# Both normalisations of the first part on ScalarE (scale and bias per row) in place of VectorE

## The chip, the core and the metric

The kernel runs on one core of a Trainium2 chip. Time is the device time of one launch in microseconds (us); lower is better. The core's engines are TensorE (PE; its weight loads are listed as PEld), VectorE (DVE), ScalarE (ACT), GpSimd (POOL) and SyncE (SP), which here only issues DMAs. Each engine runs its own instruction stream in order; the streams meet at semaphores that the program sets by hand.

## The reference

Two transformer layers on 4 x 512 rows of 256 channels, in float32:

```python
x = x + tanh(g_xattn[0]) * L0_xattn(layernorm(x), ctx)     # softmax over 16x16 per row
x = x + tanh(g_ffn[0])   * L0_ffn(layernorm(x))            # shared expert + one of 8 experts
x = x + tanh(g_xattn[1]) * L1_xattn(ctx, ctx, layernorm(x))
x = x + tanh(g_ffn[1])   * L1_ffn(layernorm(x))            # butterfly feed-forward

def layernorm(x, eps=1e-5):
    return (x - mean(x)) / sqrt(var(x) + eps)
```

The first attention is odd: for each row, queries, keys and values are split into 16 heads of 16, and the 16 x 16 scores are formed between the channels of a head, within that one row, so they are no TensorE work: they are element products of 128 x 4096 and sums of these. The change touches the first two layernorms only.

## The kernel before, in words

**Parts.** The first part (first attention, second normalisation, shared expert, router logits) runs over 16 tiles of 128 rows. Then come the routing tables, the expert part (23 tiles of rows gathered by expert), the folding of the butterfly weights, and the last part (second attention and feed-forward). The first part and the routing fill about 335 us of the trace.

**Software pipeline of the first part.** Every engine walks through steps (`sweep_a`). In step k it works on tile k (`t0`: load, first normalisation, keys, values, queries), tile k-1 (`t1`: scores, exp, attention products), k-2 (`t2`: attention sums), k-3 (`t3`: output product, second normalisation, logits) and k-4 (`t4`: shared expert). Steps 0 to 5 are written out, steps 6 to 15 are a hardware loop of two steps per pass, whose waits compare with registers, step 16 is written out, and `drain` holds the rest by hand.

**Order on each engine in a full step.**

- VectorE (`step`, L1445): product for scores L1348, gate product `mult` L1548, score sums L1357, `mult` L1548, residual add L1367, `bn_stats` L1372 for the first normalisation of t0 and the second of t3, row maximum L1387, moments `bn_aggr` L1377 (twice), shift L1396, variance + eps L1382 (twice), sums of exp L1404, XH = normalised rows of t3 (L1414), XN = normalised rows of t0 (L1484), reciprocal L1421, attention sums L1426 (two halves), scaling L1434, residual add L1442.
- GpSimd: the power -1/2 for t3 (L507) and t0 (L514), which makes 1/sqrt(var + eps), and then for t1 the attention products in two halves, each a product L529 and a halving add L531. A half waits until VectorE has read the same half of the tile before (`av_read`).
- ScalarE (`step`, L1151): gelu half (L1135), copy of the transposed attention (L1139), gelu half, copy of keys and values KV (L1165), exp (L1172), copy of transposed XH (L1144), copy of transposed XN (L1178), logits copy (L1149). Gelu and exp need different tables: there is one ACT_TABLE_LOAD ahead of each in a step.
- TensorE: transposes of the attention rows (into bank 3), output product, up product half, keys and values, down product, transposes of XH, transposes of XN, gate product (L766), query product with WQ, up product half of t3.
- SyncE: for tile t, first the store of the XH rows of tile t-5 (`keep_rows`, waits for `xn2_ready`), then the loads of tile t.

A small tensor MV holds for each of the two normalisations (index r = 0, 1) mean, variance, variance + eps and the reciprocal root, one value per row (partition). XN has one buffer, XH two.

**Drain.** After step 16, tiles 14 and 15 still have their second normalisation ahead of them, and tiles 13 to 15 the shared expert; VectorE, TensorE and ScalarE each have a written order. GpSimd computes the root of tile 14 between the two halves of its last attention products, the root of tile 15 at the end, and then issues the loads of butterfly coefficients.

Of the kernel before, what the change touches and what calls it, by code (L numbers as in the profile page):

```python
# [27 lines left out]
P = 128  # L28
# [25 lines left out]
def build(nc, x, ctxT, gates, wq0, wkv0, wo0, wg, wexp, wk1, wv1, wq1, wo1, bv1, bq1, bo1,  # L54
          weT, be, uplow, uphigh, upb, dnlow, dnhigh, wc, bc, db, out):
    with ExitStack() as ctx:
        start, twins = {}, {}

        def sb(name, shape, dt=F32):
            start[name] = (nc.sbuf_base + 31) // 32 * 32  # L60
            return ctx.enter_context(nc.sbuf_tensor(name, shape, dt))
# [13 lines left out]
        def sem(name):  # L75
            return ctx.enter_context(nc.semaphore(name))
# [51 lines left out]
        ST = sb("ST", [P, 2, 6])  # L128
        MV = sb("MV", [P, 2, 4])
        SM = sb("SM", [P, 2, DK])  # L130
        RI = sb("RI", [P, DK])
        LG = sb("LG", [P, T, NE])
        G = sb("G", [P, F])
# [117 lines left out]
        oh_ok h1_done h2_done gelu_done mult_done y_done y_added av_prod av_half recip""".split()  # L251
        s = {n: sem(n) for n in names}
        picked = sem("picked")
        route = sem("route")
        held = sem("held")
        rank_ps = sem("rank_ps")
# [869 lines left out]
        def _(act):  # L1126
            act.wait_ge(wg_in, 48)
            act.activation(TG[:, :], GATE[:, :], ACT.Tanh).then_inc(tanh_s, 1)

            def gelu(t4, hf):  # L1130
                n = 2 * num(t4) + hf
                act.wait_ge(s["h1_done"], n + 1)
                if not first(t4, 1):
                    act.wait_ge(s["mult_done"], n - 1)
                act.activation(G[:, hf * 512:(hf + 1) * 512], PB[6][:, :], ACT.Gelu).then_inc(s["gelu_done"], 1)  # L1135
# [15 lines left out]
            def step(of):  # L1151
                t0, t1, t3, t4 = of(0), of(1), of(3), of(4)
                if t4 is not None:
                    gelu(t4, 0)
                if t3 is not None:
                    attended(t3)
                if t4 is not None:
                    gelu(t4, 1)
                if t0 is not None:
                    n = num(t0)  # L1160
                    act.wait_ge(s["kv_done"], n + 1)
                    if not first(t0, 2):
                        act.wait_ge(s["qk_prod"], n - 1)
                        act.wait_ge(s["av_prod"], 2 * n - 2)
                    act.activation(KV[:, t0[1], :], PB[4][:, :], ACT.Copy).then_inc(s["kv_sb"], 1)  # L1165
                if t1 is not None:
                    n1 = num(t1)
                    act.wait_ge(s["shifted"], n1 + 1)
                    if not first(t1, 2):
                        act.wait_ge(s["av_prod"], 2 * n1 - 2)  # L1170
                        act.wait_ge(s["sums"], n1 - 1)
                    act.activation(PR[:, t1[1], :], SC[:, :], ACT.Exp, scale=float(DK) ** -0.5)\  # L1172
                        .then_inc(s["exp_done"], 1)
                if t3 is not None:
                    normal_rows(t3)
                if t0 is not None:
                    act.wait_ge(s["xT_done"], num(t0) + 1)
                    act.activation(XT[:, :, :].rearrange("p k t -> p (k t)"), PB[1][:, 0:D], ACT.Copy)\  # L1178
                        .then_inc(s["xT_sb"], 1)
                if t3 is not None:  # L1180
                    logits(t3)

            def drain():

                a, b, c = tile(T - 3), tile(T - 2), tile(T - 1)
                gelu(a, 0)
                attended(b)
                gelu(a, 1)
                normal_rows(b)
                logits(b)  # L1190
                gelu(b, 0)
                attended(c)
                gelu(b, 1)
                normal_rows(c)
                logits(c)
                gelu(c, 0)
                gelu(c, 1)
# [137 lines left out]
        def _(dve):  # L1335
# [37 lines left out]

            def moments(t, r, nm):

                hold(s[nm + "_stats"], num(t) + 1)
                dve.bn_aggr(MV[:, r, 0:2], ST[:, r, :]).then_inc(s[nm + "_agg"], 1)  # L1377

# [22 lines left out]
            def exp_sums(t2):  # L1401
# [1 line left out]
                dve.wait_ge(s["exp_done"], num(t2) + 1)  # L1403
                dve.tensor_reduce(SM[:, 1, :], PR[:, t2[1], :].rearrange("p (i j) -> p i j", i=DK),  # L1404
                                  AX.X, ALU.add).then_inc(s["sums"], 1)

            def normal_rows(t3):

                n3 = num(t3)
                dve.wait_ge(s["ln2_rstd"], n3 + 1)  # L1410
                if not first(t3, 2):
                    dve.wait_ge(s["x2T_done"], n3 - 1)
                    dve.wait_ge(xh_out[t3[1]], 16 * t3[0])
                dve.tensor_scalar(XH[:, t3[1], :], X[:, n3, :], MV[:, 1, 0:1], MV[:, 1, 3:4],  # L1414
                                  ALU.subtract, ALU.mult).then_inc(s["xn2_ready"], 1)

            def attended(t2):

# [26 lines left out]
            def step(of):  # L1445
                t0, t1, t2, t3, t4 = of(0), of(1), of(2), of(3), of(4)
                if t1 is not None:
                    scores(t1)
                if t4 is not None:
                    mult(t4, 0)  # L1450
                if t1 is not None:
                    score_sums(t1)
                if t4 is not None:
                    mult(t4, 1)
                if t3 is not None:
                    add_attended(t3)
                if t0 is not None:
                    hold(tile_in[t0[1]], 32 * t0[0] + 32)
                    stats(t0, 0, "ln1")
                if t3 is not None:  # L1460
                    hold(s["x1_ready"], num(t3) + 1)
                    stats(t3, 1, "ln2")
                if t1 is not None:
                    row_max(t1)
                if t0 is not None:
                    moments(t0, 0, "ln1")
                if t3 is not None:
                    moments(t3, 1, "ln2")
                if t1 is not None:
                    shift(t1)  # L1470
                if t3 is not None:
                    guarded(t3, 1, "ln2")
                if t0 is not None:
                    guarded(t0, 0, "ln1")
                if t2 is not None:
                    exp_sums(t2)
                if t3 is not None:
                    normal_rows(t3)
                if t0 is not None:
                    n0 = num(t0)  # L1480
                    dve.wait_ge(s["ln1_rstd"], n0 + 1)
                    if not first(t0, 1):
                        dve.wait_ge(s["xT_done"], n0)
                    dve.tensor_scalar(XN[:, :], X[:, n0, :], MV[:, 0, 0:1], MV[:, 0, 3:4],  # L1484
                                      ALU.subtract, ALU.mult).then_inc(s["xn_ready"], 1)
                if t2 is not None:
                    attended(t2)
                if t4 is not None:
                    add_shared(t4)
# [9 lines left out]
            def drain():  # L1499
# [2 lines left out]
                mult(a, 0)  # L1502
                second_norm(b)
                exp_sums(c)
                normal_rows(b)
                mult(a, 1)
                attended(c)
                add_shared(a)
                mult(b, 0)
                second_norm(c)  # L1510
                normal_rows(c)
                mult(b, 1)
                choices()
                add_shared(b)
# [419 lines left out]
```

## Time and profile before

| | us |
|---|---|
| median of 3 runs (lowest to highest) | 845.53 (844.35 to 851.41) |
| profiled execution | 846.31 |
| its span in the trace | 844.5 |
| busy: TensorE | 748.2 (89%) |
| busy: VectorE | 493.5 (58%) |
| busy: GpSimd | 390.1 (46%) |
| busy: ScalarE | 262.0 (31%) |

Busy shares are means over the whole span; a TensorE that is busy is not TensorE at its peak, since the ends of pipelined matmuls are modelled. "Idle before" in a row is the time its engine stood still ahead of the instruction, with what ended that time. The granted clock (PEclk) is the share of TensorE's full clock of 2.4 GHz; its two levels are 1.2 and 2.4 GHz. Two neighbouring instructions of one engine may overlap by about 0.1 us in the trace.

### The profile page before, as it was taken

To read this page: it belongs to the slowest core of one execution; us is meant where nothing else is said; L and a number is where in the kernel's file an instruction comes from. 1 tells how busy PE (TensorE), PEld (TensorE's weight loads), DVE (VectorE), ACT (ScalarE), POOL (GpSimd) and SP (SyncE) were. 2 spreads that over 40 slices of the span, in tenths; PEclk is the share of its full clock that TensorE was granted. 3 is DMA by queue.
4 is the path that set the end of the run, shared out by engine and by line. 5 is a ranking of instruction groups with operands and counts; after the bars stand their busy time and mean duration, and the time that the engine had idled before them with its cause. 6 is when DMAs were issued, how large, how long until landed. Compare 5 with 4: busy or idle time off the path is not lost.

```text
span 844.5 us, 11772 instructions
## 1 busy us (share of the span) xinstructions
PE 748.2 (89%) x4083; PEld 583.8 (69%) x4083; DVE 493.5 (58%) x821; ACT 262.0 (31%) x498; POOL 390.1 (46%) x326
## 2 busy tenths in 40 slices
PE   4259999999999797999999999999966889899996
PEld 1138877887888686566666666666656789799996
DVE  4889999999999737321211111111165677977652
ACT  1023333333433210122221222222132545456543
POOL 1688998898899844343333333332024141410000
PEclk9569999999999998899999999999998899999999
DMA  7000001000192017104044405000010101000000
GB/s 249 12 19 20 19 20 35 22 19 19 39 308 122 13 47 218 71 19 175 19 169 169 173 26 224 26 21 16 9 38 13 38 26 51 19 18 16 14 14 26
DMA packets 30637, 54.29 MB, mean 64 GB/s; under 512 B 9972, under 2 KB 26148, under 8 KB 29440
## 3 DMA queue, kind: packets, MB, share of 16 engines
q1 hardware_dynamic: 23168, 42.41, 14.2%
q0 software_dynamic: 4112, 8.26, 3.9%
q10 hardware_dynamic: 3312, 3.02, 1.0%
q8 instruction: 29, 0.48, 0.2%
q14 instruction: 16, 0.13, 0.1%
HBM read 46.45 MB, written 7.21 MB: 64 GB/s over the span
## 4 chain that ended last, share of the span: by engine, by line
PE 43%; DVE 11%; issue 6%; ACT 5%; DMA 2%; POOL 1%; ACTq 0%; DVEq 0%; POOLq 0%
PE bank L702 31%; PE bank L961 8%; PE bank L709 3%; DVE SLOT_r L1686 1%; DMA expert_rows<-YS 1%; DVE SLOT L1762 1%; DVE PRODV_r L1686 1%; ACT L1271 1%; POOL PRODQ L552 1%; DVE STC L1747 1%; DVE NM L1797 1%; ACT XS L1271 1%; DMA XS<-normal_rows,INV 1%; ACT SLOT_r L1275 1%; ACT SLOT L1284 1%
## 5 line engine op out<-in xcount | busy, mean ns | idle before, releaser
L702 PE MATMUL bank<-SLOT,XST 128*128 x368 | 164.6, 601 | 0.0
L529 POOL TENSOR_TENSOR PRODV<-SHARED 128x2048 f32<-128x2048 f32 x32 | 144.4, 4513 | 27.9 <-DVE bank L1426 27.9
L702 PE MATMUL bank<-SLOT,HA 128*128 (+1 forms) x624 | 146.2, 388 | 3.3 <-DVE HA L1548 2.0
L702 PEld LDWEIGHTS bank<-SLOT,HA 128*128 128x128 f32 x624 | 120.1, 194 | 38.3 <-issue 12.4
L702 PEld LDWEIGHTS bank<-SLOT,XST 128*128 128x128 f32 x368 | 69.2, 193 | 78.9 <-issue 78.8
L702 PEld LDWEIGHTS bank<-X2T,SLOT 128*128 128x128 f32 x1024 | 121.1, 195 | 1.6
L702 PE MATMUL bank<-X2T,SLOT 128*128 128x128 f32 x1024 | 121.4, 278 | 0.0
L1655 DVE TENSOR_TENSOR SHARED<-bank,G 128x512 f32<-128x512 f32 x46 | 31.8, 692 | 135.0 <-PE bank L702 135.0
L564 POOL DMA_INDIRECT XS<-normal_rows,INV x23 | 23.6, 1025 | 138.6 <-PE bank L709 121.8
L679 POOL TENSOR_TENSOR RS<-VE,MHALF 128x2 f32<-128x2 f32 x16 | 13.2, 823 | 148.3 <-DVE VE L1754 148.3
L1348 DVE TENSOR_TENSOR PRODQ<-bank,SHARED 128x4096 f32<-128x4096 f32 x16 | 70.7, 4418 | 12.6 <-PE bank L702 12.6
L531 POOL TENSOR_TENSOR PRODV<-PRODV 128x1024 f32<-128x1024 f32 x32 | 74.7, 2334 | 2.5
L1357 DVE TENSOR_REDUCE bank<-PRODQ 128x256 f32<-128x4096 f32 x16 | 70.7, 4420 | 0.1
L1646 DVE COPY HA<-bank 128x512 f32<-128x512 f32 x23 | 15.9, 692 | 72.8 <-PE bank L709 72.8
L1220 ACT ACTIVATE G<-bank 128x512 f32<-128x512 f32 x46 | 27.5, 597 | 94.0 <-PE bank L702 94.0
L961 PE MATMUL bank<-SLOT_r,PRODQ_r 128*128 128x256 f32 x256 | 47.8, 286 | 1.4 <-DVE SLOT_r L1686 1.4
L961 PEld LDWEIGHTS bank<-SLOT_r,PRODQ_r 128*128 128x128 f32 x256 | 40.7, 193 | 2.4 <-DVE SLOT_r L1686 1.6
L1226 ACT ACTIVATE YS<-bank 128x256 f32<-128x256 f32 x23 | 8.8, 384 | 106.2 <-PE bank L702 91.0
L1135 ACT ACTIVATE G<-bank 128x512 f32<-128x512 f32 x32 | 19.1, 597 | 69.1 <-PE bank L702 69.0
L702 PE MATMUL bank<-WKV,SHARED 128*128 128x512 f32 x64 | 34.5, 667 | 6.7 <-DMA WKV<-wkv 6.7
L672 POOL DMA_INDIRECT SLOT<-expert_rows,POS x16 | 16.0, 1000 | 50.1 <-DMA expert_rows<-YS 46.4
L1426 DVE TENSOR_REDUCE bank<-PRODV 128x128 f32<-128x1024 f32 x32 | 36.7, 1191 | 0.5 <-POOL PRODV L531 0.5
(243 smaller groups left out, 1368.9 us busy)
## 6 DMA issues: line engine op xcount, KB each, us to landing
SLOT<-wexp SPq DMA_DIRECT2D x9, 3072.0 KB, 11.6
expert_rows<-YS ACTq DMA_DIRECT2D x23, 128.0 KB
X<-x SPq DMA_DIRECT2D x16, 128.0 KB, 2.2
SHARED<-ctxT SPq DMA_DIRECT2D x16, 128.0 KB, 2.3
normal_rows<-XH SPq DMA_DIRECT2D x16, 128.0 KB, 1.7
WET<-ctxT SPq DMA_DIRECT2D x4, 512.0 KB, 8.2
out<-X SPq DMA_DIRECT2D x16, 128.0 KB, 1.7
WET<-weT SPq DMA_DIRECT2D x1, 1024.0 KB, 6.4
```

The lines of the kernel that those rows point to most:

```text
L529: gp.tensor_tensor(o, pr, v, ALU.mult).then_inc(s["av_prod"], 1)
L531: gp.tensor_tensor(o[:, :, :, 0:DK // 2], o[:, :, :, 0:DK // 2], o[:, :, :, DK // 2:DK], ALU.add).then_inc(s["av_half"], 1)
L564: gp.indirect_dma_start(out=XS[:, n % 2, :], out_offset=None, in_=xs, in_offset=bass.IndirectOffsetOnAxis(ap=INV[:, n:n + 1], axis=0))\
L702: last = pe.matmul(dst, lhs(k), rhs(k), start=(k == 0), stop=(k == chunks - 1))
L709: last = pe.transpose(bank[:, k * P:(k + 1) * P], src[:, k * P:(k + 1) * P], IDENT[:, :])
L961: last = pe.matmul(dst, f32r(a), f32r(b), start=(k == 0 and n == 0), stop=(k == chunks - 1 and n == 2))
L1135: act.activation(G[:, hf * 512:(hf + 1) * 512], PB[6][:, :], ACT.Gelu).then_inc(s["gelu_done"], 1)
L1220: act.activation(G[:, hf * 512:(hf + 1) * 512], PB[1 + hf][:, :], ACT.Gelu)\
L1348: dve.tensor_tensor(PRODQ[:, :].rearrange("p (i j h) -> p i j h", i=DK, j=DK), spread(PB[1][:, 0:D].rearrange("p (i o h) -> p i o h", i=DK ...
L1357: dve.tensor_reduce(SCP.rearrange("p (i j) -> p i j", i=DK), PRODQ[:, :].rearrange("p (i j h) -> p i j h", i=DK, j=DK), AX.X, ALU.add)\
L1426: dve.tensor_reduce(aov[:, :, hf * H2:(hf + 1) * H2], PRODV[:, :].rearrange("p (f i h j) -> p f i h j", f=2, i=DK, h=H2) [:, hf, :, :, 0:D ...
L1655: dve.tensor_tensor(HB[:, t1[1], hf * 512:(hf + 1) * 512], PB[3 + hf][:, :], G[:, hf * 512:(hf + 1) * 512], ALU.mult).then_inc(e["b_mult"], 1)
```

## The change

XN and XH are no longer computed by VectorE as (x - mean) * rstd. ScalarE computes them as Identity(rstd * x + bias) with bias = -mean * rstd, both per row. The bias takes two small ScalarE instructions: SHIFT[0] = -mean, and SHIFT[1] = SHIFT[0] * rstd. Semaphores order the three (`mean_neg`, `mean_rstd`), since an instruction may not read what its predecessor has not finished. In a step ScalarE does them behind the exp: the second normalisation (t3), then the first (t0), ahead of its two copies of transposed rows; in the drain behind the second gelu half. VectorE's `moments` now waits until the rows of the tile before have been normalised, since MV is overwritten.

```diff
+        SHIFT = sb("SHIFT", [P, 2, 2])
...
+            def normalise(t, r, nm, dst, signal):
+                n = num(t)
+                act.wait_ge(s[nm + "_agg"], n + 1)
+                act.activation(SHIFT[:, r, 0:1], MV[:, r, 0:1], ACT.Copy, scale=-1.0).then_inc(mean_neg[r], 1)
+                act.wait_ge(mean_neg[r], n + 1)
+                act.wait_ge(s[nm + "_rstd"], n + 1)
+                act.activation(SHIFT[:, r, 1:2], SHIFT[:, r, 0:1], ACT.Copy, scale=MV[:, r, 3:4])\
+                    .then_inc(mean_rstd[r], 1)
+                act.wait_ge(mean_rstd[r], n + 1)
+                act.activation(dst, X[:, n, :], ACT.Identity, bias=SHIFT[:, r, 1:2], scale=MV[:, r, 3:4])\
+                    .then_inc(s[signal], 1)
+            def second_rows(t3):
+                if not first(t3, 2):
+                    act.wait_ge(s["x2T_done"], num(t3) - 1)
+                    act.wait_ge(xh_out[t3[1]], 16 * t3[0])
+                normalise(t3, 1, "ln2", XH[:, t3[1], :], "xn2_ready")
+            def first_rows(t0):
+                if not first(t0, 1):
+                    act.wait_ge(s["xT_done"], num(t0))
+                normalise(t0, 0, "ln1", XN[:, :], "xn_ready")
...
             # ScalarE, step: behind the exp of t1
+                if t3 is not None:
+                    second_rows(t3)
+                if t0 is not None:
+                    first_rows(t0)
...
             # ScalarE, drain
                 gelu(a, 1)
+                second_rows(b)
                 normal_rows(b)
...
                 gelu(b, 1)
+                second_rows(c)
                 normal_rows(c)
...
             def moments(t, r, nm):
+                if not first(t, 1):
+                    dve.wait_ge(s["xn_ready" if r == 0 else "xn2_ready"], num(t))
                 hold(s[nm + "_stats"], num(t) + 1)
...
             # VectorE: normal_rows (L1407) and its calls in step and drain are gone
-                dve.tensor_scalar(XH[:, t3[1], :], X[:, n3, :], MV[:, 1, 0:1], MV[:, 1, 3:4],
-                                  ALU.subtract, ALU.mult).then_inc(s["xn2_ready"], 1)
...
-                    dve.wait_ge(s["ln1_rstd"], n0 + 1)
-                    if not first(t0, 1):
-                        dve.wait_ge(s["xT_done"], n0)
-                    dve.tensor_scalar(XN[:, :], X[:, n0, :], MV[:, 0, 0:1], MV[:, 0, 3:4],
-                                      ALU.subtract, ALU.mult).then_inc(s["xn_ready"], 1)
```

## Rows read from the trace of the kernel before

**Rows 1.** Busy time per stretch (us, instructions), granted clock, DMA: the loop's middle

```profile
core 0: us, PE busy (x) PEld busy (x) DVE busy (x) ACT busy (x) POOL busy (x), PEclk, DMA share, GB/s
...
100.00:200.00 100.00, 95.34 (x612) 80.69 (x611) 96.16 (x127) 36.02 (x60) 87.82 (x37) 1.00 0.08 24
```

**Rows 2.** Timeline of VectorE: start us, length, line, instruction, [idle before <-releaser]

```profile
98.46 4.41 DVE L1348 TENSOR_TENSOR PRODQ<-bank,SHARED 128x4096 f32<-128x4096 f32 x1
...
199.16 4.42 DVE L1348 TENSOR_TENSOR PRODQ<-bank,SHARED 128x4096 f32<-128x4096 f32 x1
...
210.59 0.42 DVE L1396 TENSOR_TENSOR SC<-bank,SM 128x256 f32<-128x256 f32 x1
...
215.87 4.42 DVE L1348 TENSOR_TENSOR PRODQ<-bank,SHARED 128x4096 f32<-128x4096 f32 x1
...
266.03 4.41 DVE L1348 TENSOR_TENSOR PRODQ<-bank,SHARED 128x4096 f32<-128x4096 f32 x1
```

**Rows 3.** Timeline of TensorE, one loop step

```profile
213.56 0.61 PE L702 MATMUL bank<-WG,X2T 128*128 128x8 f32 x4 [0.26 <-ACT X2T L1144]
214.03 1.11 PE L702 MATMUL bank<-WQ,XT 128*128 128x256 f32 x4
...
218.54 0.38 PE L709 MATMUL bank<-IDENT,AO 128*128 128x128 f32 x2
219.40 1.13 PE L702 MATMUL bank<-WO,AT 128*128 128x256 f32 x4 [0.47 <-ACT AT L1139]
```

**Rows 4.** Groups of ScalarE's instructions, 100 to 300 us: count, busy, mean ns

```profile
L1144 ACT ACTIVATE X2T<-bank 128x256 f32<-128x256 f32 x12 | 4.6, 384 | 15.4 <-PE bank L709 14.8
...
L1149 ACT ACTIVATE LG<-bank 128x8 f32 x10 | 1.8, 178 | 5.2 <-PE bank L702 5.2
```

**Rows 5.** Timeline of ScalarE, the exp in two neighbouring loop steps

```profile
211.27 1.28 ACT L1172 ACT_TABLE_LOAD   x1 [1.38 <-DVE SC L1396]
212.56 0.42 ACT L1172 ACTIVATE SHARED<-SC 128x256 f32<-128x256 f32 x1
...
225.94 0.60 ACT L1165 ACTIVATE SHARED<-bank 128x512 f32<-128x512 f32 x1 [3.00 <-PE bank L702]
226.56 1.28 ACT L1172 ACT_TABLE_LOAD   x1
```

**Rows 6.** One line's instructions in the last part: ns min/median/max, Identity with a bias per row

```profile
L1252 ACT ACTIVATE SLOT_r<-bank,BK x16: 466/472/475, 635.2 to 799.7; 128x256 fp32r<-128x256 f32 x16
```

**Rows 7.** Timeline of ScalarE, last part: a copy (L1275) that waits for the gelus ahead

```profile
667.89 0.84 ACT L1271 ACTIVATE XS<-bank,BH 128x256 f32<-128x256 f32 x2
668.83 0.64 ACT L1275 ACTIVATE SLOT_r<-XS 128x512 fp32r<-128x512 f32 x1
```

**Rows 8.** Timeline of GpSimd: the root for XN in the same loop step

```profile
211.67 0.61 POOL L514 TENSOR_TENSOR MV<-MV,MHALF 128x1 f32<-128x1 f32 x1
```

**Rows 9.** Timelines of TensorE, VectorE and GpSimd in the drain

```profile
276.02 3.72 PE L702 MATMUL bank<-SLOT,HA 128*128 128x256 f32 x16 [1.79 <-DVE HA L1548]
...
293.22 0.69 PE L709 MATMUL bank<-IDENT,XH 128*128 128x128 f32 x2 [3.10 <-DVE XH L1414]
...
295.25 5.73 PE L702 MATMUL bank<-SLOT,HA 128*128 128x256 f32 x16
300.82 3.73 PE L702 MATMUL bank<-X2T,SLOT 128*128 128x128 f32 x32
...
288.59 4.57 DVE L1414 TENSOR_SCALAR XH<-X,MV 128x256 f32<-128x256 f32 x1 [0.34 <-POOL MV L507]
...
288.52 4.49 POOL L529 TENSOR_TENSOR PRODV<-SHARED 128x2048 f32<-128x2048 f32 x1
```

**Rows 10.** Busy time per stretch, as rows 1: the drain

```profile
290.00:300.00 10.00, 6.42 (x21) 5.02 (x20) 6.66 (x6) 0.56 (x2) 5.35 (x2) 0.66 0.04 13
```

**Rows 11.** Timelines of VectorE and TensorE in the fill

```profile
24.21 4.56 DVE L1484 TENSOR_SCALAR XN<-X,MV 128x256 f32<-128x256 f32 x1 [0.67 <-POOL MV L514]
...
58.94 0.41 DVE L1414 TENSOR_SCALAR XH<-X,MV 128x256 f32<-128x256 f32 x1 [1.21 <-POOL MV L507]
...
28.82 0.69 PE L709 MATMUL bank<-IDENT,XN 128*128 128x128 f32 x2 [12.29 <-DVE XN L1484]
```

More of the change, by code:

```diff
@@ L253, in build @@
         picked = sem("picked")
+        mean_neg = [sem("mean_neg0"), sem("mean_neg1")]
+        mean_rstd = [sem("mean_rstd0"), sem("mean_rstd1")]
         route = sem("route")
@@ L1405, in exp_sums @@
                                   AX.X, ALU.add).then_inc(s["sums"], 1)
[L1407 to L1413, printed above, removed]
-                dve.tensor_scalar(XH[:, t3[1], :], X[:, n3, :], MV[:, 1, 0:1], MV[:, 1, 3:4],
-                                  ALU.subtract, ALU.mult).then_inc(s["xn2_ready"], 1)
             def attended(t2):
@@ L1476, in step @@
                     exp_sums(t2)
[L1477 to L1480, printed above, removed]
-                    dve.wait_ge(s["ln1_rstd"], n0 + 1)
-                    if not first(t0, 1):
-                        dve.wait_ge(s["xT_done"], n0)
-                    dve.tensor_scalar(XN[:, :], X[:, n0, :], MV[:, 0, 0:1], MV[:, 0, 3:4],
-                                      ALU.subtract, ALU.mult).then_inc(s["xn_ready"], 1)
                 if t2 is not None:
@@ L1504, in drain @@
                 exp_sums(c)
-                normal_rows(b)
                 mult(a, 1)
@@ L1510, in drain @@
                 second_norm(c)
-                normal_rows(c)
                 mult(b, 1)
```

## The prediction

> **What bounds the kernel now.** I read the stretches first. The first part (attention, first feed-forward, router) fills the time up to about 335 us; in its middle VectorE is 96% busy and TensorE 95%, with TensorE's clock granted in full [rows 1]: TensorE is idle 4.7 us in 100, 0.8 in a step. So neither engine can be sped up alone for long. Then the timelines of one step of the loop over row tiles, engine by engine. From one score product to the next, VectorE takes 16.71 us (199.16 to 215.87), and over the ten loop steps (266.03 - 98.46) / 10 = 16.76 us [rows 2].
>
> The important thing is a ring that closes within every step: the score product of a tile (VectorE, L1348) needs the tile's queries (TensorE), these need the transposed normal rows XN, XN needs the variance that VectorE computes behind the previous tile's scores, and the next score product needs the queries. How much room is there? The query matmuls start at 214.03 and last 1.11, so they are done at 215.14; the score product starts at 215.87 [rows 2, 3]. The room is 0.73 us. It is VectorE that arrives late, by its own queue, and not the queries.
>
> **What is removed.** Each full step loses two VectorE instructions of about 0.41 us and the wait for GpSimd's root ahead of them; VectorE would then be free well under 16 us after its score product. That by itself gives at most those 0.73 us in a step, since the ring is next, and TensorE, 95% busy, has about as little to give.
>
> **What is added.** ScalarE gets six instructions in a full step, three for each normalisation, chained by semaphores. Durations: a copy of 256 columns takes 384 ns, one of 8 columns 178 [rows 4]. The exp, the same width read from SBUF, takes 0.42 [rows 5], so SBUF costs about 0.03 more. An Identity with one operand per row takes 472 ns against 384: 0.09 for such an operand [rows 6, 4]. Hence 0.20 for the sign change, 0.29 for the product with one row operand, and 0.384 + 0.03 + 2 x 0.09 = 0.59 for the normalisation with two. A dependent ScalarE instruction starts 0.10 after its predecessor ended (668.83 against 667.89 + 0.84) [rows 7]. One normalisation is 0.20 + 0.10 + 0.29 + 0.10 + 0.59 = 1.28 us; two of them 2.46 after overlap, 2.36 counted from the end of the exp ahead (independent neighbours overlap by about 0.1). Where the price could be other: the least is the same six without any row operand and with hops of 0.03, 1.5 us a step; the most is hops of 0.26, the delay from the end of VectorE's shift (210.59 + 0.42) to the table load that waits for it (211.27), where further waits trail [rows 2, 5], 3.0 us. I take 2.36, because the row with an own-engine hop is the nearest.
>
> **Where it stands in ScalarE's queue.** Behind the exp, ahead of the two copies of the transposed rows. In one kind of loop step the table load for the exp starts only after VectorE's shift, at 211.27, and the exp runs from 212.56 to 212.98, that is 13.82 us after the step's score product; the root is there at 211.67 + 0.61 = 212.28, earlier, so the exp and not the root gates the new work [rows 5, 8, 2]. In the other kind the load follows the KV copy at once (225.94, then 226.56) [rows 5]. The kinds alternate, five of each in the loop; the two full steps before the loop are of the early kind.
>
> Late kind: XN is ready at 13.82 + 2.36 = 16.18 us. Then 0.04 to the transposes, 0.86 from the transposes through a ScalarE copy to the product (218.54 to 219.40, the same pattern on the attention output), and 1.11 + 0.04 to the next score product [rows 3]: 16.18 + 2.05 = 18.22. Early kind: the KV copy starts 11.91 us after the query matmuls (225.94 against 214.03), and with the room gone these start 1.15 before the score product, so at 10.76; copy, load and exp take 0.60 + 0.02 + 1.28 + 0.01 + 0.42, to 13.09. XN is ready at 15.45, the next score product at 17.49.
>
> So steady steps get longer: 5 x (18.22 - 16.76) + 7 x (17.49 - 16.76) = 7.3 + 5.1 = 12.4 us. The VectorE time that was taken out is then idle, since VectorE waits for the queries. TensorE is late next: it waits for XN, 1 to 1.5 us in each step.
>
> **The stalls that go.** In the drain one normalisation on VectorE took 4.57 us instead of 0.41. It started at 288.59, just behind a GpSimd product that started at 288.52 and ran 4.49, and ended when that had ended [rows 9]. The Trainium skill ("SBUF — State Buffer", Who interferes with whom) says that such a VectorE instruction and a GpSimd one take one port pair as an exclusive lock, and that ScalarE waits for no one there; the rows agree in the first half, and no row shows the second. TensorE stood 3.10 us for it, and its clock fell to the lower level, 1.2 GHz, for part of that stretch (mean 0.66 of full): the 16 down matmuls took 5.73 against 3.72 [rows 9, 10]. Without the stall the root is there at about 288.57, ScalarE's last two instructions need 0.03 + 0.29 + 0.10 + 0.59, ready 289.58; TensorE is free at 293.22 - 3.10 = 290.12 and does not wait. From there 0.86, 0.47 for four gate matmuls (213.56 to 214.03), and 3.56 for the down matmuls give 295.0 for the next up product, which now starts at 300.82 [rows 3, 9]: 5.8 us gained. The other two drain normalisations become 0.6 longer under cover of the matmuls ahead of their transposes. Routing, GpSimd's weight loads (issued behind the last root) and the expert part follow in the same order and move along.
>
> In the fill the same stall: XN of the second tile took 4.56 from 24.21, and the transposes began at 28.82 [rows 11]. With ScalarE they can begin at 24.18 + 0.03 + 0.29 + 0.10 + 0.59 + 0.04 = 25.23 (24.18 is the root's end, 0.03 ahead of that row): 3.59 earlier. The next fill step gives 0.57 back (0.29 + 0.10 + 0.59 against one 0.41 after the root). The one after pays about 1.3 for two chains, but VectorE's 1.21 us wait for GpSimd there [rows 11] mostly goes, because GpSimd's products now run earlier: 0.3. Together 2.7 gained.
>
> **What costs nothing.** The new VectorE wait ahead of the moments asks for the normalised rows of the tile before, done nearly a step earlier; if they were late, bn_aggr and all behind it would wait. SyncE's store of XH and the tile load queued behind it start about a microsecond later; the load is two tiles ahead. GpSimd starts its products when the attention sums are read, about 1 us sooner; nobody waits for it then.
>
> **Sum.** 12.4 - 5.8 - 2.7 = +3.9 us on the profiled execution's 846.3 (span 844.5): 850.2. That execution lies 0.8 above the median of 845.5, so for the median 849 to 850; I say 850.
>
> **Rivals.**
> 1. The chain on ScalarE is covered and only the stalls go: 846.3 - 2.7 - 5.8 = 837.8. The room of 0.73 in each of 12 steps would make it 829, but TensorE is idle just 0.8 in a step, and most of that is the reply time of ScalarE's copies. For it: VectorE is the busiest engine, loses work and a wait, and ScalarE is a third busy. Against: the room in the ring is 0.73 us, and the exp's end alone already leaves too little. Chance 0.12.
> 2. Slower: the four own-engine hops in a step cost 0.26 instead of 0.10, as the wait ahead of the late table load does (its waits are computed from registers in the loop). 4 x 0.16 x 12 = 7.7 more: 858. It decides from a hop of about 0.18. Chance 0.20.
> 3. ScalarE is held by GpSimd's products too, or the drain's gain is lost at a transfer that doesn't move: then 12.4 stands against little, 856 to 859. Chance 0.09.
> 4. The clock: TensorE's new waits of 1 to 1.5 us lower it. A wait of 1.79 us ahead of the down matmuls at 276.02 left them at their full 3.72 [rows 9], at full clock, so I give this nothing of its own.
> The Trainium skill ("ScalarE: Activation LUTs", Rules for kernel authors) says outright to put adds and multiplies on VectorE. The row bears it out for one instruction, 0.59 by my estimate against 0.41, and by that rule the change would lose; what it leaves out is the stall that only VectorE's version meets.
>
> **Numbers.** Forecast 0.59, rival 1 0.12, rivals 2 and 3 0.29. The least price (1.5 us a step in place of 2.36) gives 850 - 0.86 x 12 = 840, the highest 858, so 840 to 859. A measurement can tell about 1% from no change, 8.5 us: faster than 837 is rival 1 in part and a little of the low end, 0.12; above 854 are rivals 2 and 3, less their mild cases, plus the forecast's upper end, 0.27; between 0.61.
>
> **What would show it.** Loop steps of 17.5 and 18.2 us in alternation between L1348's starts, with VectorE waiting for TensorE ahead of it and TensorE for ScalarE's XN; ScalarE's three instructions near 0.20, 0.29 and 0.59, hops of 0.10; no normalisation above 0.7 us; the drain's down matmuls at 3.7 us. It is wrong if the steps stay at 16.7 (ring misread), if hops are longer, if Identity needs a table load of its own (in the last part it needs none), or if the kinds of step change.

## The result: 3.4% slower

| us | before | after |
|---|---|---|
| median (lowest to highest) | 844.94 (839.68 to 851.41) | 872.40 (870.24 to 879.09) |
| profiled execution | 846.31 | 870.24 |
| its span | 844.5 | 868.4 |

The ratio after to before is 1.0335, 95% interval 1.0243 to 1.0426. All ratios here and below are worked out from the fast executions alone (of experiment 1 that leaves out the one of 866.79), so they need not be the quotient of the medians. The forecast was 850, range 840 to 859: the time lies outside it and above every rival.

**A correction first.** The description of the change and the prediction both say that ScalarE does the two normalisations *behind* the exp. That is a misreading of the diff. They stand behind the copy of keys and values and *ahead* of the wait for the shifted scores, the table load and the exp:

```diff
                     act.activation(KV[:, t0[1], :], PB[4][:, :], ACT.Copy).then_inc(s["kv_sb"], 1)
+                if t3 is not None:
+                    second_rows(t3)
+                if t0 is not None:
+                    first_rows(t0)
                 if t1 is not None:
                     n1 = num(t1)
                     act.wait_ge(s["shifted"], n1 + 1)
```

The prediction worked out the cost of another kernel than the one that ran. The experiments hold both orders, so its numbers can be tested against the order that they were meant for.

The page of after, first busy time by engine, then the granted clock in 40 slices:

```profile
span 868.4 us, 11903 instructions
...
PE 754.7 (87%) x4083; PEld 592.5 (68%) x4083; DVE 476.4 (55%) x789; ACT 292.8 (34%) x594; POOL 389.6 (45%) x326
...
PEclk8569999999999999799999999999998999999999
```

VectorE has 17 us less work and ScalarE 31 more, and neither share says why the kernel is 24 us longer. The same stretch as [rows 1] shows where to look:

```profile
100.00:200.00 100.00, 87.62 (x526) 75.22 (x527) 79.69 (x96) 39.92 (x82) 76.66 (x31) 0.94 0.07 20
```

VectorE fell from 96% to 80% busy, TensorE from 95% to 88%, GpSimd from 88% to 77%: in the loop nobody is busy any more, so everybody waits for somebody. The clock, 1.00 in [rows 1], is 0.94.

**Where the 23.9 us of span lie,** by the starts of the score product (L1383, before L1348) and of the first transposes of the expert part:

| stretch | before | after | difference | forecast |
|---|---|---|---|---|
| fill: start of the score product of step 1 | 13.48 | 14.58 | +1.10 | none |
| fill: first to fourth score product (three spacings) | 50.05 | 47.73 | -2.32 | -2.7 |
| the two full steps before the loop | 34.93 | 39.21 | +4.28 | +1.5 |
| ten loop steps (mean 16.76 and 19.48) | 167.6 | 194.8 | +27.3 | +10.9 |
| score product of step 16 (the last) to the first expert transposes | 68.85 | 66.51 | -2.34 | -5.8 |
| from there to the end | 509.6 | 505.5 | -4.1 | 0 |

The last row is the same code on the same data sizes, and among the profiled executions below it took 503.5 to 510.5, so I read nothing into it. The loop is the case. One loop step on ScalarE, as in [rows 5]:

```profile
230.61 0.60 ACT L1194 ACTIVATE SHARED<-bank 128x512 f32<-128x512 f32 x1 [3.07 <-PE bank L705]
...
232.20 0.29 ACT L1140 ACTIVATE SHIFT<-SHIFT,MV 128x1 f32<-128x1 f32 x1 [0.88 <-POOL MV L510]
232.63 0.60 ACT L1143 ACTIVATE XH<-X,SHIFT,MV 128x256 f32 x1
233.14 0.19 ACT L1137 ACTIVATE SHIFT<-MV 128x1 f32<-128x1 f32 x1
233.36 0.29 ACT L1140 ACTIVATE SHIFT<-SHIFT,MV 128x1 f32<-128x1 f32 x1
233.78 0.60 ACT L1143 ACTIVATE XN<-X,SHIFT,MV 128x256 f32 x1
234.40 1.28 ACT L1205 ACT_TABLE_LOAD   x1
235.70 0.42 ACT L1205 ACTIVATE SHARED<-SC 128x256 f32<-128x256 f32 x1
236.02 0.36 ACT L1173 ACTIVATE X2T<-bank 128x256 f32<-128x256 f32 x1
```

Read it from the top: ScalarE stands 0.88 us for the root (L510), normalises twice, and only then loads the exp table. The copy of transposed XH (L1173) waits behind all of it. The same step on TensorE, as in [rows 3], GpSimd (with the step before), as in [rows 8], and VectorE, as in [rows 2], in this order:

```profile
217.94 5.36 PE L705 MATMUL bank<-X2T,SLOT 128*128 128x128 f32 x32
...
234.44 0.44 PE L712 MATMUL bank<-IDENT,XN 128*128 128x128 f32 x2 [0.35 <-ACT XN L1143]
236.44 0.61 PE L705 MATMUL bank<-WG,X2T 128*128 128x8 f32 x4 [1.56 <-ACT X2T L1173]
236.90 1.11 PE L705 MATMUL bank<-WQ,XT 128*128 128x256 f32 x4
...
211.66 0.55 POOL L510 TENSOR_TENSOR MV<-MV,MHALF 128x1 f32<-128x1 f32 x1 [1.25 <-DVE MV L1419]
...
216.38 4.50 POOL L532 TENSOR_TENSOR PRODV<-SHARED 128x2048 f32<-128x2048 f32 x1 [3.66 <-ACT SHARED L1205]
...
227.86 2.34 POOL L534 TENSOR_TENSOR PRODV<-PRODV 128x1024 f32<-128x1024 f32 x1
231.56 0.55 POOL L510 TENSOR_TENSOR MV<-MV,MHALF 128x1 f32<-128x1 f32 x1 [1.36 <-DVE MV L1419]
...
236.36 4.52 POOL L532 TENSOR_TENSOR PRODV<-SHARED 128x2048 f32<-128x2048 f32 x1 [3.74 <-ACT SHARED L1205]
...
218.14 4.42 DVE L1383 TENSOR_TENSOR PRODQ<-bank,SHARED 128x4096 f32<-128x4096 f32 x1 [2.83 <-PE bank L705]
...
223.41 0.69 DVE L1564 TENSOR_TENSOR HA<-bank,G 128x512 f32<-128x512 f32 x1 [0.84 <-PE bank L705]
...
238.05 4.42 DVE L1383 TENSOR_TENSOR PRODQ<-bank,SHARED 128x4096 f32<-128x4096 f32 x1 [2.84 <-PE bank L705]
```

GpSimd is the row to see. Between its root at 231.56 and its next product at 236.36 it stands 3.74 us for ScalarE's exp. So a second ring has closed: GpSimd's products, GpSimd's roots, ScalarE's two normalisations, table load, exp, GpSimd's products. They follow one another. TensorE stands 1.56 us for the copy that is held behind the exp, in every loop step; the up product that follows takes 5.36 us instead of 3.73 here, with a mean granted clock of 0.68 over it, so part of it ran at the lower level. In seven of the ten loop steps this product took 4.49 to 5.36 us, in three 3.73. VectorE's gate product then waits 0.84 us for it, and the root 1.36 for VectorE: in such a step the old ring, through the queries and the scores, has become the longer of the two, and both share the stretch from the root to the exp. What GpSimd waited for in the loop (100 to 280 us; total, times, longest):

```profile
POOL PRODV L532 <- ACT SHARED L1205: 37.0, 10, 4.0
POOL MV L510 <- DVE MV L1419: 7.7, 6, 1.4
```

The stalls of [rows 9, 11] are gone. Fill on ScalarE and TensorE, then the drain on TensorE, ScalarE and GpSimd:

```profile
11.35 0.60 ACT L1143 ACTIVATE XN<-X,SHIFT,MV 128x256 f32<-128x256 f32 x1
...
26.34 0.69 PE L712 MATMUL bank<-IDENT,XN 128*128 128x128 f32 x2 [8.89 <-ACT XN L1143]
...
312.02 0.61 PE L705 MATMUL bank<-WG,X2T 128*128 128x8 f32 x4 [1.56 <-ACT X2T L1173]
...
324.66 3.70 PE L705 MATMUL bank<-SLOT,HA 128*128 128x256 f32 x16
...
322.63 0.60 ACT L1143 ACTIVATE XH<-X,SHIFT,MV 128x256 f32<-128x256 f32 x1
...
321.81 4.50 POOL L532 TENSOR_TENSOR PRODV<-SHARED 128x2048 f32<-128x2048 f32 x1
```

XH took 0.60 us on ScalarE wholly inside a GpSimd product (321.81 to 326.31), where VectorE had needed 4.57, and the down matmuls take 3.70 again. The Trainium skill ("SBUF — State Buffer", Who interferes with whom) says that ScalarE waits for no one there; this row agrees, which no row of before could show. The first row shows a cost that I had not priced: the XN of the first tile is done at 11.95, and TensorE waits 1.74 us for it (VectorE had it at 5.53, before TensorE came to it), because on ScalarE it stands behind the KV copy.

### The profile page after: what moved, and what is told of

The parts are those of the page before. It is cut to its first block, busy times and chain, and to the rows that moved or that the text cites. A ratio compares the mean times of both kernels' runs of the same rounds, so it can differ in the third digit from the quotient of the medians.

```text
span 868.4 us, 11903 instructions
## 1 busy us (share of the span) xinstructions
PE 754.7 (87%) x4083; PEld 592.5 (68%) x4083; DVE 476.4 (55%) x789; ACT 292.8 (34%) x594; POOL 389.6 (45%) x326
## 4 chain that ended last, share of the span: by engine, by line
PE 45%; POOL 19%; issue 15%; DVE 10%; ACT 9%; DMA 2%; ACTq 0%; POOLq 0%; DVEq 0%
PE bank L705 32%; POOL PRODV L532 13%; PE bank L964 8%; PE bank L712 3%; POOL PRODV L534 3%; ACT L1205 2%; DVE SLOT_r L1702 1%; DMA expert_rows<-YS 1%; DVE SLOT L1778 1%; DVE PRODV_r L1702 1%; POOL PRODQ L555 1%; POOL MV L510 1%; ACT SHIFT L1140 1%; ACT L1306 1%; DMA XS<-normal_rows,INV 1%
## 5 line engine op out<-in xcount | busy, mean ns | idle before, releaser
L705 PE MATMUL bank<-SLOT,HA 128*128 (+1 forms) x624 | 143.2, 383 | 2.0 <-DVE HA L1564 1.1
L705 PEld LDWEIGHTS bank<-X2T,SLOT 128*128 128x128 f32 x1024 | 133.2, 211 | 2.2
L705 PE MATMUL bank<-X2T,SLOT 128*128 128x128 f32 x1024 | 132.8, 293 | 0.0
L1383 DVE TENSOR_TENSOR PRODQ<-bank,SHARED 128x4096 f32<-128x4096 f32 x16 | 70.8, 4425 | 57.2 <-PE bank L705 57.2
L1662 DVE COPY HA<-bank 128x512 f32<-128x512 f32 x23 | 15.9, 692 | 72.8 <-PE bank L712 72.8
L1164 ACT ACTIVATE G<-bank 128x512 f32<-128x512 f32 x32 | 19.1, 597 | 68.8 <-PE bank L705 68.7
```

The source lines that it names most:

```text
L705: last = pe.matmul(dst, lhs(k), rhs(k), start=(k == 0), stop=(k == chunks - 1))
L1383: dve.tensor_tensor(PRODQ[:, :].rearrange("p (i j h) -> p i j h", i=DK, j=DK), spread(PB[1][:, 0:D].rearrange("p (i o h) -> p i o h", i=DK ...
```

## The experiments

Times are medians (lowest to highest, number of runs); ratios are to the kernel before, run on the same chip alongside (845.08 in the first group of runs, 845.33 in the second).

**1. The order that I had predicted.** The two normalisations of a step go behind the exp; all else is the changed kernel.

```diff
                     act.activation(KV[:, t0[1], :], PB[4][:, :], ACT.Copy).then_inc(s["kv_sb"], 1)
-                if t3 is not None:
-                    second_rows(t3)
-                if t0 is not None:
-                    first_rows(t0)
                 if t1 is not None:
...
                     act.activation(PR[:, t1[1], :], SC[:, :], ACT.Exp, scale=float(DK) ** -0.5)\
                         .then_inc(s["exp_done"], 1)
                 if t3 is not None:
+                    second_rows(t3)
+                if t0 is not None:
+                    first_rows(t0)
+                if t3 is not None:
                     normal_rows(t3)
```

> ScalarE does its two normalisations behind the exp instead of ahead of it, all else as in the changed kernel: this is the order that the forecast had assumed. Theory Q (the ring of the queries sets the step, and the table load and exp, 1.7 us, stand in it between XN and the copy of the transposed XN): steps of 17.5 to 18.2 us, about 850 us; if TensorE's clock still falls in its waits and delays the gate products by up to 1.2 us a step, up to 864. Theory G (GpSimd's ring sets the step: products wait for the exp, the exp for the roots, the roots for the products): also faster, since the exp no longer waits for a root, about 850. Theory P (the added ScalarE instructions are the whole cost, wherever they stand): 870.

Measured: 858.15 (853.87 to 866.79, 4), ratio 1.0195 (1.0149 to 1.0240). The order is worth 14 us by the medians, 12 by the ratios. The time lies inside the forecast's range, 840 to 859, but at its upper end and not for the forecast's reasons: its loop step is 18.68, not 17.86. TensorE in one step, and the middle of the loop:

```profile
222.95 0.44 PE L712 MATMUL bank<-IDENT,XH 128*128 128x128 f32 x2 [0.86 <-ACT XH L1143]
224.10 0.44 PE L712 MATMUL bank<-IDENT,XN 128*128 128x128 f32 x2 [0.71 <-ACT XN L1143]
...
226.39 4.96 PE L705 MATMUL bank<-X2T,SLOT 128*128 128x128 f32 x32
```

```profile
100.00:200.00 100.00, 90.80 (x548) 76.82 (x549) 84.10 (x99) 40.51 (x82) 79.72 (x32) 0.95 0.07 20
```

Two short waits (0.86 and 0.71 us) stand ahead of an up product that takes 4.96 us. In the loop the second wait comes in every step, the first is 0.86 in one step and 0.20 in the next, and only the up product behind the 0.86 is slow (4.46 to 5.15). Clock or chain, this run alone can't tell.

**2. The query ring or the GpSimd ring?** In the changed kernel two theories could explain a step of 19.5. By the first, the queries are late, since the copies of transposed rows stand behind the exp. By the second, the exp is late, and GpSimd's products with it. Moving the copies ahead of the exp (the same lines are gone behind it) helps the first and hurts the second.

```diff
                 if t0 is not None:
                     first_rows(t0)
+                if t3 is not None:
+                    normal_rows(t3)
+                if t0 is not None:
+                    act.wait_ge(s["xT_done"], num(t0) + 1)
+                    act.activation(XT[:, :, :].rearrange("p k t -> p (k t)"), PB[1][:, 0:D], ACT.Copy)\
+                        .then_inc(s["xT_sb"], 1)
                 if t1 is not None:
...
```

> ScalarE's order is normalisations, copies of the transposed XH and XN, and only then the exp. Theory Q: the load and the exp leave the ring of the queries, steps shorten by about 1.4 us against the changed kernel, 853 to 857 us. Theory G: the exp ends still later, GpSimd's products start 0.8 later against their roots, ring 13.75 + 0.55 + 2.2 + 0.8 + 1.75 = 19.05 us a step and more: 866 to 872. The two theories part by over 10 us here.

Measured: 879.83 (878.09 to 884.22, 4), ratio 1.0428 (1.0392 to 1.0463): slower than the changed kernel's 872.40. But the time alone misleads here. The loop step is 19.56 against 19.48, so the first theory's 1.4 us a step didn't come, and the step hardly grew either. Most of the added time lies behind the last score product: 73.5 us to the first expert transposes against 66.5, where TensorE waited 13.03 us for the first gather of rows in place of 3.86 (the transfer of experiment 3). The waits of GpSimd and ScalarE, 100 to 290 us:

```profile
POOL PRODV L532 <- ACT SHARED L1211: 46.6, 10, 4.9
...
ACT SHARED L1194 <- POOL PRODV L532: 18.0, 4, 4.7
```

GpSimd waits 4.7 us per step for the exp instead of 3.7. What I had not foreseen is the second row: the KV copy, which writes a buffer that GpSimd's products still read, now waits for these in every second step, so that short steps (18.5 to 19.2) and long ones (19.7 to 21.0) alternate. GpSimd waits for nothing but the exp in this loop: here its ring sets the step.

**3. Only the two stalls.** The kernel before, with two of its 32 normalisations on ScalarE: XN of the second tile (fill) and XH of tile 14 (drain). The loop stays as it was. The edits stand in ScalarE's step and drain, then in VectorE's.

```diff
+                if t0 is not None and isinstance(t0[0], int) and num(t0) == 1:
+                    act.wait_ge(s["xT_done"], 1)
+                    normalise(1, 0, "ln1", XN[:, :], "xn_ready")
...
                 gelu(a, 1)
+                act.wait_ge(s["x2T_done"], T - 3)
+                act.wait_ge(xh_out[0], 16 * (T // 2 - 1))
+                normalise(T - 2, 1, "ln2", XH[:, 0, :], "xn2_ready")
...
-                if t0 is not None:
+                if t0 is not None and not (isinstance(t0[0], int) and num(t0) == 1):
...
-                normal_rows(b)
```

> The kernel before, with two normalisations alone on ScalarE: XN of the second tile (fill) and XH of tile 14 (drain), the two that took 4.5 us on VectorE. Forecast's terms: 3.6 us in the fill and 5.8 in the drain, 9.4 together, 835.5 us. Rival: the time is given back at GpSimd's products or at the first gather of rows, then nothing or only one of them shows: 840 to 845.

Measured: 840.63 (835.29 to 846.64, 12), ratio 0.9950 (0.9916 to 0.9984). Faster than both kernels, by 0.5% against the kernel before with an interval just clear of 1, but by half of what the stalls are worth, as the rival had it. The first part did gain: its last down matmuls start at 316.35 instead of 326.08. Then most of this is lost at a transfer. The kernel before and this one, on TensorE, GpSimd (the first gather of expert rows) and SyncE (the next load of expert weights, 3 MB):

```profile
326.08 5.39 PE L702 MATMUL bank<-SLOT,HA 128*128 128x256 f32 x16
...
334.88 0.69 PE L709 MATMUL bank<-IDENT,XS 128*128 128x128 f32 x2 [3.41 <-DMA XS<-normal_rows,INV]
...
327.69 1.07 POOL L564 DMA_INDIRECT XS<-normal_rows,INV  x1 [9.32 <-DVE INV L1609]
...
331.49 0.33 SPq L450 DMA_DIRECT2D SLOT<-wexp  x1
```

```profile
316.35 3.70 PE L704 MATMUL bank<-SLOT,HA 128*128 128x256 f32 x16
...
333.47 0.69 PE L711 MATMUL bank<-IDENT,XS 128*128 128x128 f32 x2 [13.42 <-DMA XS<-normal_rows,INV]
...
317.96 1.07 POOL L566 DMA_INDIRECT XS<-normal_rows,INV  x1 [9.32 <-DVE INV L1628]
...
320.08 0.33 SPq L452 DMA_DIRECT2D SLOT<-wexp  x1
```

The gather is issued 9.7 us earlier and its rows come only 1.4 us earlier: TensorE waits 13.42 us for them instead of 3.41. The weight load is issued once the last down matmuls are done; they are 1.7 us shorter with the clock kept, so it follows the gather by 2.1 us and no longer by 3.8. Of the 7.3 us between the two profiled executions only 1.4 lie ahead of the expert transposes; 5.9 lie behind them, where the code is the same, and no run shows why.

**4. Is it the clock in the changed kernel?** Seven useless matmuls (14 in the trace) between the transposes of XN and the gate product, where TensorE waits 1.56 us.

```diff
                     flip(PB[1], XN[:, :], s["xT_done"])
+                if t3 is not None and t0 is not None:
+                    for _ in range(7):
+                        pe.matmul(PB[5][:, D:D + P], IDENT[:, :], IDENT[:, :], start=True, stop=True)
                 if t3 is not None:
                     gate(t3)
```

> The changed kernel with seven matmuls without use (128x128 by 128x128, results in a half of a bank that nobody reads) on TensorE between the transposes of XN and the gate product of each full step, where it waits 1.56 us for ScalarE. Theory K (TensorE's lower clock after its waits delays both gate products on VectorE, 1.2 us a step, in series with the ring): up products back at 3.7 us, steps 1.2 us shorter, 857 to 860 us. Rival (the clock hits only work with room): granted clock up, time within 2 us of the changed kernel's 872.

Measured: 862.98 (861.73 to 864.22, 4), ratio 1.0213 (1.0185 to 1.0241): work added, 9.4 us less than the changed kernel's median, and less gained than theory K had it (857 to 860). The middle of the loop, TensorE in one step, and what GpSimd waits for from 100 to 280 us:

```profile
100.00:200.00 100.00, 94.06 (x635) 81.93 (x634) 84.77 (x98) 42.10 (x83) 80.28 (x33) 1.00 0.07 20
```

```profile
208.28 1.73 PE L798 MATMUL bank<-IDENT 128*128 128x128 f32 x14
210.01 0.61 PE L705 MATMUL bank<-WG,X2T 128*128 128x8 f32 x4
...
211.42 3.73 PE L705 MATMUL bank<-X2T,SLOT 128*128 128x128 f32 x32
```

```profile
POOL PRODV L532 <- ACT SHARED L1208: 37.0, 10, 4.0
```

The clock is 1.00 and every up product in the loop 3.73. The root no longer waits for VectorE; the wait for the exp is exactly what it was, 37.0 us. The step is 18.57, 0.91 shorter. That is the GpSimd ring by itself: its four instructions of products take 13.75 us, and from the root to the next product 4.72 pass (211.66 to 216.38 in one loop step of after), together 18.47. The last down matmuls of the first part start 12.2 us earlier than after's (341.40 against 353.63) but the first gather is then late as in experiment 3 (TensorE waits 13.82 us), so that the expert transposes come only 4.0 earlier; the rest of the difference lies in the part behind them, for which no run shows a cause.

**5. The predicted order with the clock kept.** Experiment 1, with two filler matmuls ahead of the transposes of XH and three ahead of those of XN.

```diff
+                def idle_work(bank, k):
+                    for _ in range(k):
+                        pe.matmul(bank[:, D:D + P], IDENT[:, :], IDENT[:, :], start=True, stop=True)
+
                 if t3 is not None:
+                    if t0 is not None:
+                        idle_work(PB[3], 2)
                     normal_rows(t3)
                 if t0 is not None:
+                    if t3 is not None:
+                        pe.wait_ge(s["qk_prod"], n)
+                        idle_work(PB[1], 3)
                     pe.wait_ge(s["xn_ready"], n + 1)
```

> As behind_exp (normalisations behind the exp), with five matmuls without use on TensorE in each full step, two ahead of the transposes of XH and three ahead of those of XN, where it waits up to 0.9 and 0.7 us for ScalarE. In behind_exp every second step's up products took 4.5 to 5.2 us against 3.73, and its loop steps averaged 18.68 against the 17.86 that the forecast had for this order. Theory K (what is missing in the forecast's steps is TensorE's lower clock alone): all up products at 3.7, loop steps of 17.9, about 850 us. Rival (the forecast's other terms are too small): steps stay at 18.4 and more, 856 or above.

Measured: 856.32 (850.80 to 858.79, 4), ratio 1.0163 (1.0102 to 1.0223). VectorE's score product in two neighbouring steps, and TensorE:

```profile
203.31 4.42 DVE L1392 TENSOR_TENSOR PRODQ<-bank,SHARED 128x4096 f32<-128x4096 f32 x1 [1.95 <-PE bank L705]
...
221.49 4.42 DVE L1392 TENSOR_TENSOR PRODQ<-bank,SHARED 128x4096 f32<-128x4096 f32 x1 [2.51 <-PE bank L705]
...
221.28 3.73 PE L705 MATMUL bank<-X2T,SLOT 128*128 128x128 f32 x32
```

The steps alternate between 17.53 and 18.18, mean 17.86. The forecast had 17.49 and 18.22, mean 17.86. So for this order the chain was priced right, and not by errors that cancel: of its stations, the KV copy of the early kind starts 10.77 us after the score product (forecast 10.76), XN is ready at 15.39 and 16.04 (15.45 and 16.18). And the 0.82 us that experiment 1 had on top is the clock. The median missed the expected 850 and improved only by 1.8 us, within the runs' spread: TensorE waited 8.93 us for the first gather, which the load followed by 2.1 us as in experiment 3, and took back part of the gain.

**6. The GpSimd ring without a table load.** If the ring closes through the load, taking the load out must shorten the step by about its length. The first part's gelu is computed as Tanh, which shares a table with Exp here; this changes what is computed.

```diff
-                act.activation(G[:, hf * 512:(hf + 1) * 512], PB[6][:, :], ACT.Gelu).then_inc(s["gelu_done"], 1)
+                act.activation(G[:, hf * 512:(hf + 1) * 512], PB[6][:, :], ACT.Tanh).then_inc(s["gelu_done"], 1)
```

> The changed kernel with Tanh in place of Gelu in the first part's shared expert (a change of what is computed): Tanh and Exp need no table load between them, so the 1.28 us load ahead of each exp is gone. Theory Q (the load stands in the ring, between XN and the copy of the transposed XN): steps shorter by 1.3 us, and TensorE's wait ahead of the gate product falls from 1.56 to about 0.3, so some of the clock's 0.9 us comes back: 850 to 857. If the load were covered: 872.

Measured: 851.46 (843.61 to 854.72, 10), ratio 1.0079 (1.0043 to 1.0115). GpSimd's only wait from 100 to 280 us:

```profile
POOL PRODV L532 <- ACT SHARED L1205: 25.0, 11, 2.6
```

The step is 17.16. The ring without the load and its gap is 18.47 - 1.29 = 17.18. The clock is back too (granted 1.00 from 100 to 200 us, every up product in the loop 3.73), so the step to compare with is experiment 4's 18.57, not 19.48. The load stands in the ring of the queries as well; that it is GpSimd's ring which sets this step rests on that sum and on its only wait. Even with no table load in it, the ring is longer than the old step of 16.76.

**7 and 8. The stalls, and the gather ahead of the weights.** The kernel of experiment 3, where SyncE issues that weight load only once the first two gathers have landed; and the kernel before with the same two lines.

```diff
             sp.wait_ge(s["y_done"], T)
+            sp.wait_ge(xs_in[0], 16)
+            sp.wait_ge(xs_in[1], 16)
             sp.dma_start(SLOT[:, 2, :], wexp[2]).then_inc(slot_in[2], 16)
```

> As two_stalls (840.6 us), and SyncE's load of the third expert's weights (3 MB, slot 2) waits until the first two gathers of rows have landed. In two_stalls TensorE was done with the first part 11 us sooner than before, but the first gather landed 13.4 us later than TensorE was ready, against 3.4: the weight load had been issued 2.1 us behind the gather instead of 3.8. Theory L (the two share the DMA engines and the gather loses): gather 6 to 8 us sooner, 833 to 835 us. Rival (the gather waits in GpSimd's own queue behind the coefficient loads): no gain, 840.

> The kernel before with that hold of the weight load alone. Theory L: its gather already landed early in the trace, so little, 842 to 845 us (0 to 3 us gained). If the hold itself costs (weights late for the third expert), slower than 845.

Measured: with both, 833.93 (829.54 to 836.28, 6), ratio 0.9885 (0.9838 to 0.9931); the hold alone 844.45 (839.58 to 847.76, 12), ratio 0.9999 (0.9971 to 1.0027). The first on GpSimd, TensorE and SyncE:

```profile
316.17 1.07 POOL L568 DMA_INDIRECT XS<-normal_rows,INV  x1 [9.35 <-DVE INV L1630]
...
324.26 0.69 PE L713 MATMUL bank<-IDENT,XS 128*128 128x128 f32 x2 [6.00 <-DMA XS<-normal_rows,INV]
...
324.62 0.33 SPq L454 DMA_DIRECT2D SLOT<-wexp  x1
```

The first expert transposes start at 324.26, against 333.47 in experiment 3 and 334.88 before. From the gather's issue to these transposes it took 7.2 us before, 15.5 in experiment 3 and 8.1 with the hold. The hold is worth nothing where the load was 3.8 us behind the gather, and where it was 2.1 behind 6.7 us by the medians, 5.5 by the ratios. This is the best version of all, 1.2% under the kernel before.

## Why the prediction was wrong

**The step that failed** is "Where it stands in ScalarE's queue. Behind the exp, ahead of the two copies of the transposed rows". It stands ahead of the exp. The term that hung on it, +12.4 us for twelve steps, measured 27.27 + 4.28 = +31.55. A second term failed with it: rival 4, the clock, was put at nothing. By loop step, from the runs:

| kernel | loop step, us | what it adds |
|---|---|---|
| before | 16.76 | |
| experiment 5: normalisations behind the exp, clock kept | 17.86 | 1.10, the forecast |
| experiment 4: ahead of the exp, clock kept | 18.57 | 0.71, the order |
| after | 19.48 | 0.91, the clock |

Over the twelve steps, between the same runs, the 31.55 are 11.0 for the predicted order (forecast 12.4), 8.9 for the real order and 11.7 for the clock. So of the 19.1 us that are missing, the clock is the larger part, and it is missing in the predicted order too.

**A second ring was overlooked.** I followed one ring (scores, variance, XN, queries, scores) and asked of GpSimd only when its products start and who waits for them. But the two roots stand behind the products in its queue, and the exp that starts the next products now stands behind what the roots release. Such a ring has no slack: 13.75 us of products and 4.72 from root to product. Experiments 2, 4 and 6 move the step to 19.56, 18.57 and 17.16, as this sum demands (in experiment 2 it takes 5.63 to 5.88 us from root to product: 19.4 to 19.6). In the changed kernel itself the root waits up to 1.4 us for VectorE in six of the steps between 100 and 280 us, so there the ring of the queries, lengthened by the clock, is the longer one; GpSimd's is what is left when the clock is kept. Had I read the diff rightly, a chain of "root, two normalisations, load, exp" against a GpSimd that is 88% busy [rows 1] would have pointed to it.

**Rival 4, the clock, was given nothing and is worth 0.91 us a step** (experiment 4), and 0.82 in the predicted order (1 against 5). The slow up products of the changed kernel's ten loop steps alone are 8.9 us longer than 3.73 each, 0.89 a step. It was set aside on one row, a single wait of 1.79 us in the drain after which the matmuls kept their speed [rows 9]. In the loop, waits of 0.25 to 0.67 and of 1.56 us come in every step, and in seven steps of ten the up product that follows takes 4.49 to 5.36 us. A row of one wait doesn't bear out a rule for waits that recur.

**The drain, -5.8, was right where it was read, but not in total.** From the up product of one tile to that of the next (before 286.38 to 300.82, after 319.60 to 328.20) the time went from 14.44 to 8.60: 5.84 gained. But "the other two drain normalisations become 0.6 longer under cover" is not all that happens. In step 16 XH, load and exp again stand ahead of the copy that TensorE needs, with a wait of 1.56 us and an up product of 5.45 behind it: from the last score product to the first of the two up products named above it took 23.24 us in place of 20.35, so 2.9 were given back, and another 0.6 between the second of them and the expert transposes.

**The fill, -2.7, was right for its stall** (3.58 in the spacing of the score products, forecast 3.59) and missed the first tile, whose XN stands behind the KV copy: +1.10.

**Rival 3's second half was a real mechanism in the wrong kernel.** After didn't lose the drain's gain at a transfer (its last down matmuls take 5.39 and the load follows the gather by 3.8 us, as before); experiments 2 to 5 lost time there (the load 2.1 us behind the gather in each).

**What was right:** ScalarE's prices (forecast 0.20, 0.29, 0.59; measured 0.20, 0.29, 0.60), that ScalarE isn't held by GpSimd's products, that VectorE's removed work buys nothing, that Identity needs no table load, and that no one waits for the normalised rows ahead of the moments. The hop was a little too dear: 0.03 to 0.04 us where the steps are written out, and 0.03 and 0.13 in the loop (233.14 + 0.19 to 233.36; 233.36 + 0.29 to 233.78), against 0.10; rival 2's 0.26 did not occur.

**Adding up,** on the profiled executions: 870.2 - 850.2 = 20.0 us of error, which is +19.1 for the steps, +1.5 for the fill (-1.2 in place of -2.7), +3.5 for the drain, and -4.1 for the rest, which the change doesn't touch.

**What stays open:** why one wait of 1.79 us left the clock alone and repeated shorter ones didn't, and why the same waits left three up products of ten at 3.73; fillers were tried in two places only. And why a gather that is issued 2.1 us ahead of a 3 MB load lands so much later than one 3.8 us ahead: that holding the load back cures it is shown, the mechanism in the transfer is not.

## What to carry to other kernels

Before moving work to an idle engine, follow what stands behind its new place in that engine's queue, and for each thing delayed ask who starts from it: here GpSimd, 88% busy, started from the exp and fed the very wait put ahead of it, and a ring closed. When a stall occurs in two places of a kernel and the work in thirty-two, move the two; then look at which transfers the earlier finish sets against each other. And short waits of TensorE that recur in every step have a price beyond their length, which a few filler matmuls showed here and partly gave back.

## What the runs showed of the hardware

- TensorE's granted clock over 100 to 200 us fell from 1.00 to 0.94 with waits of 0.25 to 0.67 and of 1.56 us in every step of 19.5 us, and to 0.95 with 0.71 in every step and 0.86 in every second one (steps of 18.7); seven fillers per step brought back 1.00 and 0.91 us a step in the first case, five 1.00 and 0.82 in the second.
- An Identity with scale and bias per row, 128 x 256 in SBUF, took 0.60 us on ScalarE inside a GpSimd product; the same work on VectorE took 4.57 us there [rows 9].
- From the issue of the first gather of expert rows to the matmuls that wait for it passed 7.2 to 8.5 us in the four traces where a 3 MB load followed it by 3.8 us, 11.0 to 15.9 in the four where it followed by 2.1, and 6.8 and 8.1 in the two where it was held back.
